# A CIN and tower kernel: a row of ids spread over the partitions by TensorE, and the start's weight loads in another order

## What is computed

```python
e = jnp.stack([tbl_0[ids[:, 0]], ..., tbl_31[ids[:, 31]]], axis=1)      # (512, 32, 32)
# for W in (filter_0, filter_1):  x0 = e, prev = e at first
z = jnp.einsum('bhd,bmd->bhmd', x0, prev).reshape(b, h * m, d)
cur = relu(jnp.einsum('bpd,pn->bnd', z, W[0]))                         # n = 128
# both layers' cur, summed over d, side by side: z (512, 256)
h = jnp.concatenate([z, dense_ctx], axis=1)                            # (512, 272)
h = jnp.maximum(h @ W_top1 + b_top1, 0.0)                              # 512 wide
h = jnp.maximum(h @ W_top2 + b_top2, 0.0)                              # 256 wide
y = h @ W_top3
```

## Time and profile before

| | |
|---|---|
| median of 3 runs | 889.67 us (888.46 to 891.25) |
| profiled execution | 889.24 us, its span 887.1 us |
| busy, share of the span | PE 95%, DVE 88%, ACT 86%, POOL 73% |
| from the span's start to PE's last long wait (L885 begins) | 51.07 us |
| from there to the end of the span | 836.0 us |

### The profile page before, as it was taken

The page is one execution under the profiler, slowest core; times in us unless marked ns, Lnnn a source line. Parts: engine busy times, 40 slices in busy tenths (PEclk is TensorE's granted clock), DMA queues, the critical chain, the costliest instruction groups (busy, mean ns, idle before and its releaser), DMA issues.

```text
span 887.1 us, 14536 instructions
## 1 busy us (share of the span) xinstructions
PE 841.0 (95%) x3637; PEld 678.5 (76%) x3637; DVE 779.7 (88%) x2420; ACT 764.0 (86%) x2582; POOL 650.2 (73%) x615
## 2 busy tenths in 40 slices
PE   0578999999999999999999999999999999999998
PEld 0346888888887888888888888888888888888873
DVE  2475999999999999999999999998899999999884
ACT  1239999999999999999999999999999999999872
POOL 6456888787788888888887888876766666676582
PEclk9979999999999999999999999999999999999999
DMA  7437767667767767667767666677767666675430
GB/s 181 106 75 199 176 155 163 147 153 170 161 153 168 163 152 163 147 157 166 162 153 174 161 154 161 144 164 160 160 154 170 155 155 156 143 165 106 92 72 0
DMA packets 53236, 131.20 MB, mean 148 GB/s; under 512 B 8395, under 2 KB 17875, under 8 KB 53028
## 3 DMA queue, kind: packets, MB, share of 16 engines
q0 software_dynamic: 21872, 68.43, 43.0%
q1 hardware_dynamic: 29502, 59.08, 20.3%
q10 hardware_dynamic: 1779, 2.77, 1.1%
HBM read 60.63 MB, written 3.05 MB: 72 GB/s over the span
## 4 chain that ended last, share of the span: by engine, by line
PE 89%; SPq 3%; DVE 3%; ACT 2%; DMA 2%; issue 1%; DVEq 0%
PE ya L870 14%; PE ya L872 14%; PE ya L871 14%; PE yd L870 11%; PE yd L872 11%; PE yd L871 11%; PE acc L870 3%; PE acc L872 3%; PE acc L871 3%; SPq L315 3%; ACT scaled L541 2%; DMA xb<-xt_scratch 1%; DVE emb L658 1%; DMA idx<-in_ids 1%; PE acc L899 1%
## 5 line engine op out<-in xcount | busy, mean ns | idle before, releaser
L541 ACT ACTIVATE scaled<-ya,emb 128x128 f32<-128x128 f32 x2288 | 654.3, 382 | 53.8 <-PE ya L872 46.0
L763 DVE SCALAR_TENSOR_TENSOR acc<-yd,emb,acc 128x128 f32<-128x128 f32 x1400 | 394.4, 341 | 5.9 <-PE yd L872 5.8
L406 POOL TENSOR_TENSOR quarter<-scaled 128x512 f32<-128x512 f32 x127 | 195.2, 1537 | 64.4 <-DMA scaled<-scaled 46.9
L870 PE MATMUL ya<-w_hi,prev_hi 128*128 128x512 f32 x572 | 224.8, 393 | 4.5 <-ACT scaled L541 2.5
L872 PE MATMUL ya<-w_hi,prev_lo 128*128 128x512 f32 x572 | 222.8, 390 | 0.0
L871 PE MATMUL ya<-w_lo,prev_hi 128*128 128x512 f32 x572 | 222.8, 390 | 0.0
L399 POOL DMA_DIRECT2D scaled<-scaled x127 | 116.4, 917 | 96.4 <-ACT scaled L541 91.7
L870 PE MATMUL yd<-w_hi,prev_hi 128*128 128x512 f32 x446 | 174.3, 391 | 1.0 <-DVE pooled_b L788 1.0
L872 PE MATMUL yd<-w_hi,prev_lo 128*128 128x512 f32 x446 | 173.6, 389 | 0.0
L871 PE MATMUL yd<-w_lo,prev_hi 128*128 128x512 f32 x446 | 173.5, 389 | 0.0
L381 POOL DMA_INDIRECT emb<-in_tbl,idx x112 | 123.2, 1100 | 42.7 <-issue 22.2
(11 more groups left out here) (136 smaller groups left out, 778.0 us busy)
## 6 DMA issues: line engine op xcount, KB each, us to landing
scaled<-scaled POOLq DMA_DIRECT2D x127, 512.0 KB, 8.3
xb<-xt_scratch SPq DMA_DIRECT2D x62, 512.0 KB
x<-xt_scratch SPq DMA_DIRECT2D x62, 192.0 KB
xm<-xt_scratch SPq DMA_DIRECT2D x30, 256.0 KB
scaled<-in_w ACTq DMA_DIRECT2D x4, 512.0 KB
emb<-in_tbl,idx POOLq DMA_INDIRECT x112, 3.9
xt_scratch<-xt_stage SPq DMA_DIRECT2D x7, 256.0 KB
wt_sb<-in_W_top SPq DMA_DIRECT2D x2, 512.0 KB
```

Of the source, the lines that this page charges most:

```text
L406: pool.tensor_tensor(four, piece[:, 0:C], piece[:, C:2 * C], ALU.add).then_inc(quartered, 1)
L541: op = act.activation(scaled[:, tile % PR, C * j + N * i:C * j + N * (i + 1)], a_bank(n)[:, N * i:N * (i + 1)], ACT.Copy, scale=scale_of(t ...
L763: dve.scalar_tensor_tensor(after, y_part, scale_of(tile, HB * j + i), before, ALU.mult, ALU.add).then_inc(chained, 1)
L870: pe.matmul(dst, v_hi, m_hi, start=start, stop=False)
```

## The change

Four things change.

1. `ids_across` is no longer loaded. One row of 2048 ids goes to one partition (`ids_row`). DVE casts it to float32 (`cast`), and PE multiplies it by a row of ones in four matmuls of 512 columns, which puts each id on all 128 partitions in PSUM (`across`). `find` now works from there in two halves for each tile.
2. Layer 1's weights (`w1_raw`, 2 MB in four transfers) are issued by ACT only after it has waited until the small tables have landed. The ids of tiles 1 to 3 go to ACT's queue ahead of them.
3. The tower's two large weights (`wt1_sb`, `wt2_sb`, 0.5 MB each) are issued by SP behind `load_l0(2)`, in the main loop's first chunk. A new semaphore, `ctx_loaded`, covers the two small loads that the start needs.
4. The two bias vectors and `W_top3` are laid out ahead by the host and come in one transfer of 128 x 8 (`tower_small`) in place of three of single words; `dense_ctx` comes in rows laid out by partition; the scale column `halves` comes with `pick_sb`.

```diff
+        ids_row = sb("ids_row", [1, PICK_TILES, len(SMALL) * P], I32)
+        ids_f32 = [xt_stage[0:1].rearrange("p g b -> p (g b)"), emb_sorted[0:1].rearrange("p g b -> p (g b)")]
+        across = [yd[:, 0, :], yd[:, 1, :], yd[:, 2, :], acc0[:]]
...
             sp.dma_start(idx[:, 0, :], ids[0:P, :]).then_inc(ids_loaded, 16)
+            sp.dma_start(ids_row[:], ids_first.rearrange("t f b -> (t f b)").rearrange("(o t n) -> o t n", o=1, t=PICK_TILES)
+                         ).then_inc(pick_loaded, 16)
             sp.dma_start(pick_sb[:], pick).then_inc(pick_loaded, 16)
-            sp.dma_start(ids_across[0:PICK_P], dram(ids_first, 0, [[0, PICK_P], [1, PICK_TILES * len(SMALL) * P]])).then_inc(
-                pick_loaded, 16)
...
-            sp.dma_start(idx[:, 1:BT, :], ids[P:B, :].rearrange("(t p) f -> p t f", p=P)).then_inc(later_ids_loaded, 16)
-            sp.dma_start(wt1_sb[:], W_top1[0:2 * P, :].rearrange("(t p) n -> p t n", p=P)).then_inc(tower_loaded, 16)
-            sp.dma_start(wt1_ctx[:], W_top1[2 * N:2 * N + D_CTX, :]).then_inc(tower_loaded, 16)
-            sp.dma_start(wt2_sb[:], W_top2.rearrange("(t p) n -> p t n", p=P)).then_inc(tower_loaded, 16)
-            with nc.allow_non_contiguous_dma(reason="a few hundred words, once"):
-                sp.dma_start(wt3_sb[:], W_top3.rearrange("(t p) n -> p (t n)", p=P)).then_inc(tower_loaded, 16)
-                sp.dma_start(bt1_sb[:], b_top1.rearrange("(t p) -> p t", p=P)).then_inc(tower_loaded, 16)
-                sp.dma_start(bt2_sb[:], b_top2.rearrange("(t p) -> p t", p=P)).then_inc(tower_loaded, 16)
+            sp.dma_start(wt1_ctx[:], W_top1[2 * N:2 * N + D_CTX, :]).then_inc(ctx_loaded, 16)
+            sp.dma_start(tower_small[:], biases_w3).then_inc(ctx_loaded, 16)
...
             load_l0(2)
+            sp.dma_start(wt1_sb[:], W_top1[0:2 * P, :].rearrange("(t p) n -> p t n", p=P)).then_inc(tower_loaded, 16)
+            sp.dma_start(wt2_sb[:], W_top2.rearrange("(t p) n -> p t n", p=P)).then_inc(tower_loaded, 16)
             sp.wait_ge(xt_written, 32)
...
+            act.dma_start(idx[:, 1:BT, :], ids[P:B, :].rearrange("(t p) f -> p t f", p=P)).then_inc(later_ids_loaded, 16)
+            act.wait_ge(small_tables_loaded, 16 * len(SMALL))
             for s in range(4):
                 fields = slice(s * F // 4, (s + 1) * F // 4)
                 act.dma_start(w1_raw[:, fields, :], w1[:, fields, :]).then_inc(w1_loaded, 16)
...
             for bt in range(PICK_TILES):
+                pe.wait_ge(ids_cast, bt + 2)
+                for r in range(2):
+                    pe.matmul(across[2 * bt + r], ones[:], ids_f32[bt][:, C * r:C * (r + 1)], start=True, stop=True).then_inc(
+                        ids_in_psum, 1)
```

More of the change, by code:

```diff
@@ L12, with cin_tower @@
 P = 128
-def cin_tower(nc, dense_ctx, ids, tables, W_top1, b_top1, W_top2, b_top2, W_top3,
-              w0_first, w0_second, w0_small, w1, eye, fold_scale, ids_first, pick, out):
-    B, D_CTX = dense_ctx.shape
+def cin_tower(nc, ctx_rows, ids, tables, W_top1, W_top2, biases_w3,
+              w0_first, w0_second, w0_small, w1, eye, ids_first, pick, out):
+    B, D_CTX = ids.shape[0], ctx_rows.shape[2]
     F = ids.shape[1]
@@ L629, in _, with cast @@
         def _(dve):
+            def cast(bt):
+                dve.tensor_copy(ids_f32[bt], ids_row[:, bt, :]).then_inc(ids_cast, 1)
             def find(bt):
[L632 to L636, removed]
+                for r in range(2):
+                    n = 2 * bt + r
+                    dve.wait_ge(ids_in_psum, n + 1)
+                    if n > 0:
+                        dve.wait_ge(where_made, 2 * n)
+                    dve.tensor_scalar(not_below[0:PICK_P], across[n][0:PICK_P], pick_sb[0:PICK_P, 0:1], None,
+                                      ALU.is_ge).then_inc(where_made, 1)
+                    dve.wait_ge(where_made, 2 * n + 1)
+                    dve.scalar_tensor_tensor(where[bt][0:PICK_P, C * r:C * (r + 1)], across[n][0:PICK_P], pick_sb[0:PICK_P, 1:2],
+                                             not_below[0:PICK_P], ALU.is_lt, ALU.mult).then_inc(where_made, 1)
             def number_within(bt):
@@ L660, in pick_rows @@
                                       ALU.add).then_inc(picked, 1)
+            dve.memset(ones[:], 1.0).then_inc(ids_cast, 1)
             dve.wait_ge(pick_loaded, 32)
+            cast(0)
+            cast(1)
             find(0)
@@ L671, in _ @@
             dve.wait_ge(w0_folded, 1)
-            dve.tensor_scalar(w0_a[:, 0, :], w0_a[:, 0, :], halves[:, 0:1], None, ALU.mult).then_inc(w0_folded, 1)
-            dve.wait_ge(later_ids_loaded, 16)
-            number_within(1)
+            dve.tensor_scalar(w0_a[:, 0, :], w0_a[:, 0, :], halves, None, ALU.mult).then_inc(w0_folded, 1)
             pick_rows(0)
@@ L679, in _ @@
             dve.tensor_tensor(low_third, w16[2 * F:3 * F], low_third.bitcast(F32), ALU.subtract).then_inc(w_lo_ready, 1)
+            dve.wait_ge(later_ids_loaded, 16)
+            number_within(1)
             pick_rows(1)
@@ L861, in _ @@
                         rows.then_inc(rows_in_psum, 1)
+            pe.wait_ge(small_tables_loaded, 16 * len(SMALL))
+            candidates(0)
+            pe.wait_ge(consts_loaded, 32)
+            pe.wait_ge(where_made, 8)
+            for t in range(BT):
+                turn = pe.transpose(acc0[0:D_CTX, P * t:P * (t + 1)], ctx_in[:, t, :], identity[:])
+            turn.then_inc(ctx_turned, 1)
+            candidates(1)
             pe.wait_ge(ctx_ready, 1)
-            pe.wait_ge(tower_loaded, 16 * 6)
+            pe.wait_ge(ctx_loaded, 32)
             pe.wait_ge(picked, len(PAIRS))
@@ L965, in _ @@
                             pe.wait_ge(folded0, 2 * BT)
+                            pe.wait_ge(tower_loaded, 32)
                             tower_pooled0(0)
@@ L1028, with by_partition @@
     n_fields = inputs["ids"].shape[1]
+    def by_partition(a):
+        a = np.asarray(a)
+        return a.reshape(-1, P, a.shape[1]).transpose(1, 0, 2)
     scale = np.ones((P, 1), np.float32)
     scale[::4] = 0.5
-    args = [given("dense_ctx", inputs["dense_ctx"]), given("ids", inputs["ids"]),
+    args = [given("ctx_rows", by_partition(inputs["dense_ctx"])), given("ids", inputs["ids"]),
             [given(f"tbl_{f}", inputs[f"tbl_{f}"]) for f in range(n_fields)]]
-    args += [given(n, inputs[n]) for n in ("W_top1", "b_top1", "W_top2", "b_top2", "W_top3")]
+    small_weights = [by_partition(np.asarray(inputs[n]).reshape(-1, 1))[:, :, 0] for n in ("b_top1", "b_top2", "W_top3")]
+    args += [given("W_top1", inputs["W_top1"]), given("W_top2", inputs["W_top2"]),
+             given("biases_w3", np.concatenate(small_weights, axis=1))]
     w0 = np.asarray(inputs["L0_rec_filter_0"]).reshape(n_fields, n_fields, -1)
```

48 lines of the change are left out of this document (22 added, 26 removed).

## The result

| | before | changed |
|---|---|---|
| median of 20 runs each | 889.51 us (888.18 to 891.25) | 887.41 us (885.29 to 889.88) |
| profiled execution, its span | 889.24, 887.1 us | 889.88, 886.9 us |
| first transposes on PE begin | 51.07 us | 46.60 us |

The ratio is 0.9979, with a 95% interval of 0.9972 to 0.9987: a gain of 2.1 us, within the 0.3% that the prediction called no change. Forecast were 874.7 us and a range from 872.7 to 880.0. The result lies outside it.

The account below looks back on a forecast made before the run. PE was taken to bound everything behind its first transposes (836 us), the small tables' landing to set the start. Transposes at 36.1 instead of 51.07 save 15.0: 889.24 - 15.0 = 874.2, plus 0.4 for the median, 874.7 us; range 872.7 to 880.

Parts of the forecast that it names:

- The tables' landing: Start: the small tables land at time t, between 11.9 and 14.6 us, taken as 14.6; before, 33.17.
- the rival with t past 17: Start: small tables landing after 17 us cost one us per us; 877.7 us at 20, 879.7 at 22; chance 0.18.
- The id path: Start: DVE's casts, PE's four matmuls and `find` end by about 14.5 us, hidden under the table load.
- The picking chain: Start: from the tables' landing, both tiles' picks take 18.45 us, so the last pick ends at 33.1.
- The gathers: Start, on POOL: gather 24 starts at 33.75 and lands 2.0 us later, completing tile 0's rows at 35.75, after the picks.
- the rival with them held by DVE: Start: DVE's reduces hold up POOL's gathers, the last slipping by up to 5 us, to 879.7 us; chance 0.08.
- PE's transposes at 36.1: End of the start: PE begins the embedding transposes at 36.1 us in place of 51.07, 15.0 us less.
- ACT's chain: Start: layer 1's weights land at 23.3, their split ends by 27.0 or 27.9, and ACT is free at 34.7.
- Tower weights at 0: First chunk: 1 MB of late tower weights costs at most 1.2 us, taken as 0; as rival 875.9 to 877.1, chance 0.06.
- That is if the 15 us are taken back in the main loop: Refutation sign: the forecast is wrong if PE is not already the bound behind the start.
- the premise that PE bounds what stands behind the start: Behind the first transposes: everything takes 836 us whatever came before, unless its own waits change.
- The sum: Whole kernel: 51.07 - 36.1 = 15.0 us less, nothing added behind; profiled 874.2, median 874.7 us; forecast's chance 0.62.

Follow-up runs that it names:

- wt_early: The changed kernel with the tower's two large weights issued at the start, behind SP's small loads: 874.54 us, ratio 0.9828 (chip 8).
- w1_early: The changed kernel without ACT's wait for the small tables, so layer 1's weights are issued at once: 881.96 us, ratio 0.9921 (chip 8).
- after_again: The changed kernel word for word, run a second time, on chip 0: 877.89 us, ratio 0.9871.
- after_third: The changed kernel word for word, run a third time, on chip 0: 877.40 us, ratio 0.9880.
- turn_first: The changed kernel with the context's four transposes ahead of tile 0's products in PE's list: 877.42 us, ratio 0.9868 (chip 8).
- wt_chunk6: The changed kernel with the tower's two large weights issued ahead of the loads of chunks 6 and 7, one each: 873.94 us, ratio 0.9826 (chip 0).
- both_moved: The changed kernel with context transposes first on PE and tower weights ahead of chunks 6 and 7: 874.12 us, ratio 0.9837 (chip 0).
- after_fourth: The changed kernel word for word, run a fourth time, on chip 14: 886.43 us, ratio 0.9969.
- both_moved_b: The changed kernel with context transposes first on PE and tower weights ahead of chunks 6 and 7, on chip 14: 883.46 us, ratio 0.9923.
- ids_alone: The changed kernel with both weight moves undone, leaving the ids' spreading and the packed small loads: 879.94 us, ratio 0.9896 (chip 0).
- hold_b: The changed kernel with POOL's gathers stopped after the 13th until PE's eight picking products are signalled, on chip 14: 884.21 us, ratio 0.9935.

## Why the prediction was wrong, step by step

**The tables' landing.** Right within 0.8 us: 15.41 against 14.6 (the rival with t past 17 fell in all four traces of the changed kernel, 14.88 to 15.87). In `wt_early`, with 1 MB more behind them in the queue, the first product starts at 17.0, and in `w1_early` at 21.92 beside ACT's 2 MB: sharing makes the tables late, as the earlier trace rows had it.

**The id path.** Right. Two casts of 0.68 us, PE's four matmuls from 5.38 on, the last `find` ended at 14.4, inside the table load.

**The picking chain.** Right where nothing held it: from 15.87 to 34.40 in `after_again`, 18.5 us against 18.45.

**The gathers.** Right, the rival with them held by DVE wrong. The last gather of tile 0 starts at 32.72 in the changed kernel and 32.61 in `after_again`, and all follow every 1.25 us beside DVE's reduces of 1.03 us. None slipped. The last one even starts 1.1 us before the 33.75 that the forecast had taken over from the earlier trace rows. The Trainium skill (SBUF — State Buffer, "Who interferes with whom") says that on this chip a reduce never contends with GpSimd, and these traces agree.

**PE's transposes at 36.1.** Right on chips 8 and 0 where ACT lets the tables go first and POOL is not held (35.28 to 36.04), wrong in the execution behind the result (46.60) and in its like on chip 14 (44.91). The step that failed there is "ACT's chain": "is free at 34.7" takes for granted that ACT starts once PE has done what it waits for. On these occasions ACT starts 8 to 14 us later. "The picking chain" rests on the same step: its `w_lo` needs ACT's split, and its picks need PE's signals, which came up to 16 us after their products' rows ended. No rival named it. The trace before did not show it either: there the products ran from 33.17, when POOL had one more gather to issue, and the one signal that PE gave under the gathers, that of the context's transposes from 20.48 to 21.50, had ACT start at 21.54. The change moves the products under the gathers. What the runs show: it happens with gathers of POOL in flight on one chip of three (and in the result's runs, whose chip is not given), in all executions of an occasion or in none (20 of 20 and 9 of 9 runs at 885 us or more, 9 of 9 at 880.2 or less); it vanishes when the gathers stop, it does not hang on ACT's 2 MB, and it is the signals that are held, not the products that end late. What stays open is the mechanism: what holds a signal of PE while gathers run, and whether the clock's rise has a part in it. And no run tells why chips differ.

**Tower weights at 0, "as the queues share, I take 0".** Wrong, and the error that is wholly mine. I looked for their victim in `part` on POOL and bounded the loss at 1.2 us. The victims are the loads around them in the same queue. In the result's execution and in `after_again` it is the one issued just ahead: chunk 2's 16-bit rows take 15.06 us to land in place of 11.80, DVE's small product waits 3.34 us, and PE stands still for 4.24 us from 74.37 (`after_again`). The rows were issued only 2.6 us ahead of the weights (59.31 and 61.88), and had not landed by then. In `after_third` and `turn_first` most of the wait is for chunk 3's rows. Measured: 2.6 us added to the kernel before, and 2.9 to 4.0 us taken off when they leave (turn_first to wt_early, after_again to wt_chunk6, after_third to both_moved, after_fourth to both_moved_b). That transfers share the engines did not save them, as "the queues share" had assumed.

**"That is if the 15 us are taken back in the main loop"** was named as what would refute the forecast, and a part of it happened: of the 4.5 us that the profiled execution had won at the transposes, 4.3 were gone by the end. The traces settle what took it back. From the start of the transposes to the end of the span it was 836.0 us before. It is 835.5 to 837.3 us in all five traces with the tower's weights at the start or at chunks 6 and 7 (`wt_early`, `ids_alone`, `wt_chunk6`, `both_moved`, `both_moved_b`), and 838.5 to 842.2 us in all ten with them in the first chunk. So the premise that PE bounds what stands behind the start held within 1.3 us, with late signals or without, and the weights are what broke it. In `after_again` 15.8 us were won at the transposes and 10.4 arrived at the end; 4.3 of the 5.4 lost are the weights (841.4 against 837.1 us in `wt_chunk6`).

**The sum.** With signals in time 877.4 and 877.9 were measured: inside the range, and 3 us off the number, which is what the tower's weights cost, less the 0.8 us by which the gathers ended sooner than forecast. The range had room for that by other rivals, so that it held there is in part luck. The late signals add another 8.5 to 10.0 us (`after_fourth` and the result against these two).

## What to carry to other kernels

Pulling work of one engine under another's long string of indirect gathers is a change of company, not only of time: look at what signals will now be given during them, and measure on more than one chip. When a big load is moved into a running queue, don't look for the next thing that uses an engine or a sum; take the loads issued in the 10 us or so on either side of it, find who waits for each, and what slack that waiter has. A load of weights for the end of the kernel cost nothing that shows four chunks later (873.9), and 3 to 4 us where the loop's first loads have no lead yet.

## What the runs showed of the hardware

- With gathers of POOL in flight, signals of PE came up to 16 us after the rows of the instructions that give them end, on chip 14 and in the result's trace (the first `yd` product of `both_moved_b`: row to 21.44, signal at 37.42). Held signals came in a bunch, four within 0.18 us. With the gathers stopped on chip 14 the delay was at most 1.1 us, and 0.02 us from 22.26 on (`hold_b`). On chips 0 and 8 ACT's copy of the context started within 0.1 us of the end of the transposes' row in every kernel where it was waiting for them (`after_again`: 21.63 and 21.66).
- A load of SP's queue that took 11.80 us to land in `wt_chunk6` took 15.06 us when 1 MB was issued behind it within 3 us (`after_again`), with the DMA engines full (share 1.04 from 60 to 76 us, against 0.82).
- What a standstill of PE costs beyond itself differs. In `after_again` it stood still for 4.24 us from 74.37, and the granted clock averaged 0.76 from 76 to 90 us; in `w1_early` it stood still for 2.73 us from 79.47, and the granted clock was 1.00 from 76 to 115 us.
